# Mamba scan: GpSimd scales the transposed input by B per partition, and TensorE turns it back into PSUM

## The reference, cut to what matters

```
delta = jax.nn.softplus(dt @ dtp_w.T + dtp_b)
A = -jnp.exp(A_log)
def step(h, inp):
    u_t, d_t, b_t, c_t = inp
    dA = jnp.exp(d_t[:, :, None] * A)
    h = h * dA + (d_t * u_t)[:, :, None] * b_t[:, None, :]
    y = jnp.einsum('bdn,bn->bd', h, c_t)
    return (h, y)
```

## Time and profile before

| what | value |
|---|---|
| time, median of 3 runs | 2613.18 us (2610.1 to 2615.79) |
| profiled execution, its own time | 2614.2 us |
| its span, first to last instruction | 2612.1 us |
| mean granted TensorE clock | 0.962 |
| busy: PE, DVE, ACT, POOL | 85%, 86%, 73%, 84% of the span |
| Mamba loop | about 534 to 2086 us |

### The profile page before, as it was taken

The page is one execution under the profiler, slowest core; times in us unless marked ns, Lnnn a source line. Parts: engine busy times, 40 slices in busy tenths (PEclk is TensorE's granted clock), DMA queues, the critical chain, the costliest instruction groups (busy, mean ns, idle before and its releaser), DMA issues.

```text
span 2612.1 us, 48904 instructions
## 1 busy us (share of the span) xinstructions
PE 2227.8 (85%) x15840; PEld 1908.7 (73%) x15840; DVE 2240.6 (86%) x3430; ACT 1895.3 (73%) x3628; POOL 2198.4 (84%) x1402
## 2 busy tenths in 40 slices
PE   4899999668888898888888888888988768999992
PEld 3799999446776777776776766766766647999992
DVE  8766666789999999999999999999999887666666
ACT  4355555389999989999999999999999543555551
POOL 3677777379999999999999999999999936777772
PEclk8999999889999999999999999999999978999996
DMA  7011112533333333333333333333333240111126
GB/s 249 21 48 49 49 50 50 144 94 105 110 103 104 107 106 102 107 107 101 111 101 103 112 100 105 111 107 104 106 107 107 85 161 24 50 49 49 49 49 211
DMA packets 156821, 248.73 MB, mean 95 GB/s; under 512 B 22082, under 2 KB 66018, under 8 KB 155874
## 3 DMA queue, kind: packets, MB, share of 16 engines
q1 hardware_dynamic: 137568, 202.79, 26.1%
q0 software_dynamic: 18208, 37.26, 5.3%
q10 hardware_dynamic: 866, 6.43, 0.6%
HBM read 213.10 MB, written 33.29 MB: 94 GB/s over the span
## 4 chain that ended last, share of the span: by engine, by line
PE 37%; POOL 19%; DVE 15%; issue 14%; ACT 10%; DMA 4%; ACTq 0%; DVEq 0%; POOLq 0%; SPq 0%
PE bank L1351 10%; POOL buf L548 8%; DVE buf L917 7%; PE bank L1547 6%; PE bank L1372 6%; PE bank L1422 4%; POOL token_outputs L497 4%; POOL buf L487 4%; PE bank L1522 3%; PE bank L1332 3%; ACT over L1164 3%; DMA buf<-state_rows 2%; ACT scaled L1197 2%; DVE buf L904 2%; POOL buf L535 2%
## 5 line engine op out<-in xcount | busy, mean ns | idle before, releaser
L548 POOL TENSOR_TENSOR buf<-buf 128x1024 f32<-128x1024 f32 x512 | 1199.9, 2374 | 32.4 <-PE bank L1547 27.0
L917 DVE TENSOR_TENSOR_SCAN buf<-over,bank 128x512 f32<-128x512 f32 x832 | 953.8, 1200 | 4.9 <-PE bank L1522 2.7
L1164 ACT ACTIVATE over<-wgu,negA 128x510 f32<-128x510 f32 x832 | 541.5, 709 | 40.3 <-DVE buf L917 28.8
L1547 PE MATMUL bank<-id_sb,buf 128*128 128x128 f32 x4096 | 515.8, 279 | 6.8 <-POOL buf L548 6.8
L1547 PEld LDWEIGHTS bank<-id_sb,buf 128*128 128x128 f32 x4096 | 478.2, 144 | 57.2 <-issue 46.6
L1351 PE MATMUL bank<-parts 128*128 128x256 f32 x3408 | 447.6, 288 | 17.3 <-DVE buf L767 9.2
L1351 PEld LDWEIGHTS bank<-parts 128*128 128x128 f32 x3408 | 420.7, 193 | 36.7 <-issue 36.7
L1197 ACT ACTIVATE scaled<-wd_sb,I 128x256 f32<-128x256 f32 x896 | 377.3, 497 | 22.6 <-PE bank L1522 22.5
L497 POOL DMA_INDIRECT token_outputs<-buf,slot_out x284 | 299.5, 1055 | 87.9 <-issue 84.0
L487 POOL DMA_INDIRECT buf<-token_rows,slot_token x284 | 284.5, 1002 | 95.4 <-issue 82.5
L1522 PE MATMUL bank<-id_sb,scaled 128*128 128x128 f32 x1792 | 256.0, 280 | 88.3 <-ACT scaled L1197 38.2
(11 more groups left out here) (170 smaller groups left out, 3061.6 us busy)
## 6 DMA issues: line engine op xcount, KB each, us to landing
buf<-state_rows SPq DMA_DIRECT2D x608, 256.0 KB, 3.2
token_rows<-buf SPq DMA_DIRECT2D x32, 256.0 KB, 2.3
wd_sb<-token_outputs SPq DMA_DIRECT2D x16, 512.0 KB, 4.0
buf<-token_outputs SPq DMA_DIRECT2D x16, 512.0 KB, 4.8
buf<-token_rows,slot_token POOLq DMA_INDIRECT x284, 2.5
token_outputs<-buf,slot_out POOLq DMA_INDIRECT x284
out<-X SPq DMA_DIRECT2D x16, 256.0 KB, 3.6
wgu<-wgT ACTq DMA_DIRECT2D x1, 2048.0 KB, 9.1
```

Of the source, the lines that this page charges most:

```text
L548: pool.tensor_tensor(hC[:, b, :].rearrange("p (c w) -> p c w", c=C), hs[:, b, :].rearrange("p (c w) -> p c w", c=C), Cs[:, b, :].unsqueeze ...
L917: V.tensor_tensor_scan(hs[:, b, w], dA[:, b, c, :, :].rearrange("p s t -> p (s t)"), source, 0.0, ALU.mult, ALU.add).then_inc(s[f"scan_don ...
L1164: ins = A.activation(dA[:, n % R, c, :, 1:], delta[r][:, c * W:(c + 1) * W].rearrange("p (s t) -> p s t", s=S)[:, :, 1:], ACT.Exp, scale=n ...
L1547: ins = M.matmul(bank[4 + q // 2][:, at:at + P], hC[:, n % R, c * W + q * P:c * W + (q + 1) * P], id_sb[:, :], is_transpose=True, start=Fa ...
```

## The change

For states 3, 9 and 15 the input product is made as for the turned states, by GpSimd in place of ACT. `scale_by_B` on GpSimd multiplies `duT` by the column of B that is a scalar per partition, in four `tensor_scalar` of 128x256, into `pscaled`. PE transposes it into banks 0 and 1 (`turn_back_pool`, eight transposes), at the head of its steps 2, 8 and 14, and DVE scans it in two pieces of 512 like every other state, with decays that ACT writes into SBUF three states ahead. The broadcast fetches of B (`fetch_B`), `decay_to_bank` and the scans in four pieces go. GpSimd makes the tile for 15 behind `times_C` of 7 (before: 11). ACT overwrites `duT` only when GpSimd's three groups of the unit are done, and SP loads `wd` for the last stage only when all of them are. The core of the diff:

```diff
-MUL_AT = {0: 3, 4: 9, 11: 15}
-FETCH_C, FETCH_B, DECAY_LEAD = 3, 7, 3
+MUL_AT = {0: 3, 4: 9, 7: 15}
+FETCH_C, DECAY_LEAD = 3, 3
...
-        prod = carve(rest, 2 * CW).rearrange("p (b w) -> p b w", b=2)
-        Bs = carve(rest + 2 * CW, 2 * W).rearrange("p (b w) -> p b w", b=2)
+        pscaled = carve(rest, 2 * CW).rearrange("p (b q d) -> p b q d", b=2, q=G)
...
-            def product(p, r, n):
+            def scale_by_B(p, r, n):
...
-                k, j = turn % 2, POOL_UNITS.index(n)
-                pool.wait_ge(s[f"B_in{k}"], (turn // 2 + 1) * DMA)
-                if j >= 2:
-                    pool.wait_ge(s["scan_done1"], u * NS + POOL_UNITS[j - 2] + 1)
-                else:
-                    wait(pool, s["scan_done1"], (u - 1) * NS + POOL_UNITS[j - 2] + 1)
-                pool.wait_ge(s["du_done"], u + 1)
-                pool.tensor_tensor(prod[:, k, :].rearrange("p (c w) -> p c w", c=C),
-                                   du[r].rearrange("p (c w) -> p c w", c=C),
-                                   Bs[:, k, :].unsqueeze(1).broadcast_to([P, C, W]),
-                                   ALU.mult).then_inc(s["pool_mul_done"], 1)
+                pool.wait_ge(s["BT_done"], u + 1)
+                pool.wait_ge(s["duT_done"], 2 * u + 2)
+                wait(pool, s["pturned1"], turn - 1)
+                for q in range(G):
+                    ins = pool.tensor_scalar(pscaled[:, turn % 2, q, :], duT[:, q, :], BT[:, u % 2, q, n:n + 1], None,
+                                             ALU.mult)
+                ins.then_inc(s["pscaled_done"], 1)
...
-                if on_pool(n):
-                    turn = pool_before(u, n)
-                    dve.wait_ge(s["pool_mul_done"], turn + 1)
-                    for c in range(C):
-                        dve.wait_ge(s[f"dP_ready{c}"], turn + 1)
-                        for q in range(S):
-                            w = slice(c * W + q * L, c * W + (q + 1) * L)
-                            ins = V.tensor_tensor_scan(hs[:, b, w], bank[c][:, q * L:(q + 1) * L],
-                                                       prod[:, turn % 2, w], 0.0, ALU.mult, ALU.add)
-                        ins.then_inc(s[f"scan_done{c}"], 1)
-                    return
-                dve.wait_ge(s["dA_ready"], decays_before(u, n) + 1)
+                dve.wait_ge(s["dA_ready"], N + 1)
...
+                    elif on_pool(n):
+                        dve.wait_ge(s[f"pturned{c}"], pool_before(u, n) + 1)
+                        source = bank[c]
...
-            def decay_to_bank(p, r, n):
-
-                u = p * 2 + r
-                for c in range(C):
-                    act.wait_ge(s[f"scan_done{c}"], u * NS + n - 1)
-                    A.activation(bank[c], delta[r][:, c * W:(c + 1) * W], ACT.Exp,
-                                 scale=negA[:, r, c, n:n + 1]).then_inc(s[f"dP_ready{c}"], 1)
...
                 if k == 0:
                     wait(act, s["scaled_done"], turned_before(u, 0))
+                    wait(act, s["pscaled_done"], pool_before(u, 0))
...
-                        if n + 1 < NS and on_pool(n + 1):
-                            decay_to_bank(p, r, n + 1)
                         beside(p, r, n, first, last)
                         if n + DECAY_LEAD < NS:
-                            if not on_pool(n + DECAY_LEAD):
-                                decay(p, r, n + DECAY_LEAD)
-                        elif prep and not on_pool(n + DECAY_LEAD - NS):
+                            decay(p, r, n + DECAY_LEAD)
+                        elif prep:
                             decay(pv, rv, n + DECAY_LEAD - NS)
...
+            def turn_back_pool(p, r, n):
+
+                u = p * 2 + r
+                turn = pool_before(u, n)
+                pe.wait_ge(s["pscaled_done"], turn + 1)
+                for c in range(C):
+                    wait(pe, s[f"scan_done{c}"], u * NS + n - 1)
+                    for q in range(G):
+                        ins = M.transpose(bank[c][:, q * P:(q + 1) * P], pscaled[:, turn % 2, q, c * P:(c + 1) * P],
+                                          id_sb[:, :])
+                    ins.then_inc(s[f"pturned{c}"], 1)
...
                     for n in range(NS):
                         if on_turn(n + 1):
                             turn_back(p, r, n + 1)
+                        elif n + 1 < NS and on_pool(n + 1):
+                            turn_back_pool(p, r, n + 1)
```

More of the change, by code:

```diff
@@ L101, in vector_before @@
     return (u + whole) * len(mine) + sum(m < part for m in mine)
-def decays_before(u, n):
-    return u * NSTATE + n - pool_before(u, n)
 def done(steps, name, turn):
@@ L316, in macaron_kernel @@
             experts_done expA_done dtp_zeroed diag_ready taps_spread taps_ready parts_ready skip_ready gT_pe gT_done BT_pe BT_done duT_pe duT_done scaled_done turned0 turned1 gated du_done dve_pre
-            act_pre pe_pre vareps_pre rstd_pre shift_pre res_done pe_post negA_done bcB_ready bc_copied bc_stored C_in0 C_in1 C_in2 C_in3 B_in0 B_in1 dA_ready
-            dP_ready0 dP_ready1 mul_done pool_mul_done scan_done0 scan_done1 hC_ready y_done""".split()
+            act_pre pe_pre vareps_pre rstd_pre shift_pre res_done pe_post negA_done bcB_ready bc_copied bc_stored C_in0 C_in1 C_in2 C_in3 dA_ready
+            pturned0 pturned1 mul_done pscaled_done scan_done0 scan_done1 hC_ready y_done""".split()
         s = {n: sem(n) for n in names}
@@ L383, in fetch_C @@
                              ).then_inc(s[f"C_in{n % R}"], DMA)
-            def fetch_B(u, r, n):
-                turn = pool_before(u, n)
[L387 to L392, removed]
             def pair_rows(p, last):
@@ L401, in pair_rows @@
                             fetch_C(u + 1, 1 - r, n + FETCH_C - NS)
[L402 to L406, removed]
                         if n == SP_AT["rows"] and not (last and r == 1):
@@ L412, in _ @@
                 fetch_C(0, 0, n)
-            fetch_B(0, 0, POOL_UNITS[0])
             pair_rows(0, False)
@@ L424, in _ @@
             sp.wait_ge(s["scaled_done"], turned_before(2 * NP, 0))
+            sp.wait_ge(s["pscaled_done"], pool_before(2 * NP, 0))
             sp.wait_ge(s["comb_done"], NG)
@@ L557, in pair @@
                         if n in MUL_AT:
-                            product(p, r, MUL_AT[n])
+                            scale_by_B(p, r, MUL_AT[n])
                         if r == 0 and not last and n == POOL_AT["rstd"]:
```

## The result

The changed kernel takes 2966.22 us (median of 4 runs, 2965.43 to 2967.28) where before took 2613.88 beside it: ratio 1.135, 95% interval 1.1331 to 1.137. It is 352 us slower. The prediction had the sign and the place of the loss, and gave 2808 us with a range up to 2910: the loss came out 1.8 times as large as its 194 us.

What follows compares the result with a forecast made beforehand. The prediction took full GpSimd and a closed loop from gate to gate, both 48.9 us a unit, as the bound. 4.6 us of loop plus 1.7 of clock, 6.3 in 31 units, gave 2808 us, range 2700 to 2910.

Steps and rivals of the forecast that it cites:

- The price of GpSimd's group: Time t of GpSimd's four tensor_scalar for one tile: 1.9 us, so GpSimd's work falls by 1.3 us a unit.
- The loop: Closed chain from DVE's gate through PE's sum 0 and GpSimd's times_C to the next gate: 48.9 us before.
- T to C4: DVE's gate to GpSimd's times_C of state 4: 10.9 or 9.5 us before; 0.44 and 0.12 less every other unit.
- C4 to C15: GpSimd from the start of times_C of state 4 to the end of state 15: 35.0 us before, 0.9 less after.
- C15 to T: End of GpSimd's times_C of state 15 to DVE's gate: 3.0 us before, 8.8 after, without the clock loss.
- 3t - 1.1: Growth of the loop per unit, t being GpSimd's time for one group: +4.6 us forecast, 7.6 at t of 2.9.
- The clock: PE's granted clock falls to half behind its wait for GpSimd's group: +1.7 us a unit, bounds 0 and 4.3.
- the dear rival: GpSimd's small operations take t of 2.9 us and more, with half clock: 2901 to 2981 us, chance 0.08.
- The wait's place: PE's step 2: turning state 3 waits for GpSimd ahead of the sums that DVE's gate needs, +5.8 us.
- States 9 and 15, the fetches, ACT: Transposes for 9 and 15 lie under scans, fewer fetches change nothing, ACT's 0.2 us a unit fits beside its idle.
- the gate waits but the loop through C4 stays open: DVE's gate waits, but sum 0 is ready for GpSimd's times_C of state 4: 2669 to 2722 us, chance 0.14.
- Faster: Tile for state 3 is ready when PE needs it; GpSimd's relief of 1.3 us a unit counts: 2573 us, chance 0.06.

Runs made afterwards that it cites:

- x7: Changed kernel with 32 transposes of the identity put into PE's wait ahead of turning state 3: 3110.62 us, ratio 1.1064 to before on a slower chip.
- x2_onett: Changed kernel with GpSimd's four tensor_scalar replaced by one tensor_tensor with repeated columns of B: 2765.44 us, ratio 1.0575 to before.
- x1: Changed kernel with PE's turning of state 3 moved behind the taps and sums of step 2: 2793.75 us, ratio 1.0688 to before.
- x5: Changed kernel with GpSimd's tile for state 3 made ahead of times_C of state 0: 3061.37 us, ratio 1.0896 to before on a slower chip.
- x6: Changed kernel with the eight transposes of state 3 done twice: 3199.33 us, ratio 1.1385 to before on a slower chip.
- x3: Changed kernel with one tensor_tensor per tile and the turning of state 3 behind step 2's sums: 2651.36 us, ratio 1.0143 to before.
- x10: x8 with DVE's split_lo moved from behind scan 5 to behind scan 6: 2641.8 us, ratio 1.0101 to before.
- x11: x10 with step 2's last two convolution taps behind the sums and the turning of state 3: 2643.8 us, ratio 1.0111 to before.
- x8: x3 with GpSimd's tile for state 9 made behind times_C of state 3 instead of 4: 2838.53 us, ratio 1.011 to before on a slower chip.

## Why the prediction was wrong, step by step

*The price of GpSimd's group* is the term that failed. The prediction put t, the time of one group, at 1.9 us, "the middle of memset and L478", with 2.9 as the upper bound from the product with two full operands; it measured 3.64, 3.62 from one start to the next. The prediction's own sign of being wrong, a tensor_scalar outside 0.4 to 0.72 us, came true with 0.93. GpSimd's work, which was to fall by 1.3 us a unit, rose by 3.8. The reasoning was that one operand is streamed and so the price must lie below that of two. The rows that it rested on (memset, tensor_tensor) were of other operations, and the only tensor_scalar among them, 128x16, shows the start but no slope. The Trainium skill led the same way: GPSIMD Engine Reference, section 3.1, gives 1.03 cycles an element for short loop bodies and, as a best case of a tight loop, about 1.8. The prediction took these as the range for one input; the section names neither tensor_scalar nor an upper bound. At its 1.2 GHz the copy's 0.83 ns is 1.0 cycle, in agreement; the tensor_scalar's 2.5 ns is 3.0, and the measurement decides.

*The loop* held, term by term, in the unit shown. T to C4: 9.5 less 0.56 forecast, 8.9 measured. C4 to C15: 35.0 - 0.9 = 34.1 forecast; with t at 3.6 it is 37.5, and 37.5 was measured. C15 to T: 8.8 and 1.7 of clock forecast, 1.7 more for t, 12.2; measured 1381.58 - 1369.4 = 12.2. The other direction agrees: T to C4 is 10.6 us there and C15 to T 12.4, on the mean. The prediction's sum 3t - 1.1 with t = 3.62 gives 9.8, and 1.6 of clock (x7) 11.4: 31 x 11.4 = 353 us, against 351.4 in the loop.

*The clock.* That 1.7 met the 1.6 of the changed kernel is luck. It was worked out for t = 1.9 from some 5 us of idle PE. PE's waits for GpSimd's tile between 700 and 1900 us (us in total, times, longest), in x2_onett, which has that t, and in the changed kernel:

```profile
PE bank L1491 <- POOL buf L511: 52.8, 23, 2.7
PE bank L1492 <- POOL buf L512: 88.1, 20, 4.4
```

That is 2.3 us each at t = 1.9, and 4.4 at t = 3.6. In x2 the loss over 4.6 is 0.5 a unit. So even with its t the prediction was 43 us too high: x2 takes 2765 where it says 2808. The prediction's upper bound of 4.3 for the clock is 4.5 by its own terms (0.9, 1.7 and 1.9), which would make the dear rival's 2981 us 2987.

*The wait's place*, said by the prediction (the gate behind GpSimd's tile through PE's queue), was shown by x1, x5 and x6. *States 9 and 15, the fetches, ACT:* the terms above leave nothing for them in the changed kernel, as forecast; that the transposes for 15 cost some time in a full stretch of PE is argued from x3, where the larger stalls are gone.

*Rivals.* That the small operations are dear had 0.08 and was what happened. Its 2901 to 2981 us hold the 2966, but not by its terms: t was 3.6 where it priced 2.9, and the half clock cost 1.6 us where it took up to 4.3. That the gate waits but the loop through C4 stays open is refuted by the changed kernel's trace: C4 waits for PE, and with t = 3.62 and 1.7 of clock that rival's terms give about 54 us a unit, an estimate, against the 58.6 shown. Faster is excluded for this order, as x2 is slower even with the price assumed; in the mended versions a GpSimd with less to do didn't bring the time under before's either.

What stays open is what sets the 49.2 us of x10: taking away DVE's wait for ACT (x10) and then the gate's wait for PE as well (x11) shortened nothing to speak of. And why tensor_scalar costs 2.5 ns an element on GpSimd isn't known from these runs.

## What to carry to other kernels

Before an engine gets a new kind of operation, find a row of that very operation at two sizes, or measure it; the number of operands is no bound on the price. Where an engine's queue is in order, ask of each added wait what stands behind it: here two sums had nothing to do with the tile that they waited for, and moving them brought back half of the loss. And where several engines are full at once, follow the closed loop from gate to gate rather than the busiest engine. With the measured price its terms give the changed kernel's loss within 1%. They were 43 us too high for x2_onett, and where no single loop binds (x3, x8) such sums promised gains that didn't come.

## What the runs showed of the hardware

GpSimd's tensor_scalar costs 2.5 ns an element of float32 at 256, 512 and 1024 a partition, dearer than a tensor_tensor of two full operands (2375 ns for 1024, 2.1 an element behind 0.2 us) and than one whose second operand repeats (1611 ns for 852 and 1906 for 1024, 1.7 an element); a copy of 1024 takes 1047 ns. To scale by a value per partition, the tensor_tensor with the repeated column was half the price of four tensor_scalar (1.91 us against 3.64). And work with no other use, 32 transposes in a wait of 4.4 us, kept TensorE's granted clock at 1.00 behind the wait and made the loop 49 us shorter, while without it the clock stood at 0.50 there.
